# Side work of a Mamba and feed-forward kernel placed in other units

## The chip, the cores and the metric

The kernel runs on one core of a Trainium2 chip. The metric is device time in microseconds (us), the median of several runs; a profiled execution of its own has a time beside them. The core has five engines with queues of their own: PE (TensorE, matrix products), DVE (VectorE), ACT (ScalarE), POOL (GpSimd) and SP (SyncE, which here issues every DMA). They meet through semaphores alone.

## What is computed

For each of 16 batch elements of 512 rows by 256 columns (fp32), with shift, scale and gate rows drawn from a condition vector:

```
h  = layernorm(x) * (1 + ca) + sa
xn = layernorm(h, ln1)
m  = mamba1(xn) + flip(mamba2(flip(xn)))
x  = x + ga * (layernorm(m, ln2) + xn)
h  = layernorm(x) * (1 + cb) + sb
x  = x + gb * ffn(h)        # ternary weights, hidden 1024: silu*gate, gelu, gelu, out

mamba(x): xp, z = split(x @ W_in.T)           # 512 channels each
          xc    = silu(causal conv4(xp) + conv_b)
          dt_lo, B, C = split(xc @ W_xp.T)    # 16, 64, 64
          dt    = softplus(dt_lo @ W_dt.T + dt_b)
          h_t   = exp(dt_t * A) * h_(t-1) + (dt_t * xc_t) * B_t     # 512 x 64 states
          y_t   = h_t . C_t
          out   = ((y + xc * D) * silu(z)) @ W_out.T
```

The recurrence, 512 channels by 64 states by 512 time steps in two directions, is nearly all of the work.

## The kernel before

**Units.** The scan of one batch element is cut into 128 *units*: 8 passes (2 directions by 4 blocks of 128 channels) of 16 groups of 4 states. A unit is 4 tiles of 128 partitions (32 channels by 4 states) by 512 steps, handled in two halves. For each unit ACT computes the decays (`decays`, an exp into `state`), DVE scans twice (`scan`, 128x1024 each, L1278), POOL multiplies the states by C (`read`, twice, L1308), and PE sums them over the states into the bank `y_ps` (`accumulate`, L904). What drives the scan, u times B, is made in two ways. For even units DVE multiplies (`drive`, L1267, at the end of the odd unit before), with B spread by one PE product. For odd units ACT (8 and 4 operations, L1091) and POOL (one, L1375) make `v` in a ring of two, and PE transposes it into the bank pair `driven` (`drive`, L882, two times eight transposes). ACT makes `v` five units ahead in an even unit (first part, after a wait for PE's second drive of the unit after) and the next (second part). The state ring holds four units.

**Order on PE.** In an even unit u: drive(u+1, 0), accumulate(u-1), drive(u+1, 1), spread(u+2), side work of u. In an odd unit: accumulate(u), side work of u. Where u is a multiple of 16, accumulate(u-1) comes first.

**Side work.** Everything else of the network is cut into *steps*, each written into a list for its engine with the unit at whose end it is issued. Each engine runs its list in that fixed order behind its scan work of the same unit, so a step that has to wait stops its whole engine. A mid-body of 128 units has the scan of batch element b, the early and late halves of the feed-forward network of b-1 (`early`, `late`), the projections for the second direction of b (`p1`), and the norm and the projections for the first direction of b+1 (`next`). Bodies: pre (only `next` of element 0), first, 14 times mid, last, tail (the network of the last element with no scan).

**Steps of a projection** (`projection_steps(part, s)`): T0, T1 transpose the input; X0 to X3 project; K0 to K3 are the convolution (two steps each on PE); xc is its silu; BC, CL, BT project to B and C (BC ends with a DVE step that frees its bank); D0 to D3 project dt, whose softplus is ACT's exp, one, ln and DVE's rest (two operations) and dt; ua, ub are POOL's products u = dt * xc; cut is a DVE memset that waits for ub; Z0 to Z3 project z, sz is its silu. UT0 to UT7 transpose u for `v`, one for each pass. Y steps are DVE's: they empty `y_ps` after each pass.

**Steps of the network**: O1a, O1b output projection; `o_` norm, mix, mixed, `n_` norm, N0, N1 transposes, then for each half i: F (8 steps, ACT empties each with two operations), silu, two glu on POOL, H (8 times two quarters), gelu, G (the same), gelu, W (4 steps). `FFN_AT` gives the units at which F, H, G and W begin; `norm_steps` lists stats, aggr (DVE), rstd (POOL, 9 small operations) and norm (ACT). `PRE_AT`, `MIX_AT`, `N_AT`, `X_AT`, `O0_AT`, `UT_AT` place the rest.

**Banks.** Projections, UT and O0 (list PE_P) share one PSUM bank `p_ps`, the network (list PE_Q) shares `q_ps`. `bank_free` makes PE wait until the user before in the same list has been emptied:

```
                by_dve = n in ("BC", "O1a", "O1b", "W0", "W1")
                who = dve_side if by_dve else act_side
                pe.wait_ge(who.sem, who.done(at, p, n))
```

**SP** issues in each unit, in this order: chunks of network weights, the C row of two units on (`load_c`, which waits for POOL's read of this unit), `load_u` for UT, the next pass, stores of B and C and of u and dt (`store_bc`, `store_ud`), weights (`load_wp`, `load_wdt`, `load_wout`), `load_conv`, `load_next`. A wait stops the whole queue.

## Time and profile before

| what | value |
|---|---|
| median of 3 runs | 12781.52 us (12780.62 to 12787.79) |
| profiled execution, its time | 12787.71 us |
| its span, first to last instruction | 12785.9 us |
| mean granted clock of PE | 0.901 |
| busy: DVE | 11921.9 us (93%) |
| busy: POOL | 11371.3 us (89%) |
| busy: ACT | 10826.9 us (85%) |
| busy: PE | 10149.5 us (79%) |
| one batch element (5588.53 to 6363.11) | 774.58 us |

"L1278" is line 1278 of the kernel. In a row of groups, "out<-in" gives the tiles, then the shapes, "x" the count, then busy us, mean ns of one, and the idle time of the engine ahead of it with what ended it. In the timeline a row begins with its start and its duration in us, and the bracket at its end is the idle time ahead of it and what ended that. SPq is SP's queue.

### The profile page before, as it was taken

The page shows a single profiled execution, that of the slowest core. Times are in us where ns is not written, and L with a number is a line of the kernel's source. Part 1 is how long each engine was busy: PE and PEld are TensorE (multiplying, and loading weights), DVE is VectorE, ACT ScalarE, POOL GpSimd, SP SyncE. Part 2 cuts the span into 40 slices and gives each one's busy share as a digit, 9 for nine tenths or more (in the row PEclk, how much of TensorE's full clock was granted, in tenths as well). Part 3 has the DMA queues.
Part 4 walks back from the last instruction along what each step waited for, and adds up shares of the span by engine and source line. Part 5 has one row for each costly group of instructions (what it writes and reads, how often), then busy time and mean ns, then how long its engine had stood idle before and what let it go on. Part 6 is the DMA issues. An engine that isn't in the chain of part 4 may idle for free.

```text
span 12785.9 us, 179504 instructions
## 1 busy us (share of the span) xinstructions
PE 10149.5 (79%) x51484; PEld 5801.2 (45%) x51484; DVE 11921.9 (93%) x7080; ACT 10826.9 (85%) x23460; POOL 11371.3 (89%) x5924
## 2 busy tenths in 40 slices
PE   5667878888787887877878778887878878788777
PEld 2334544444444454544445444454444545444445
DVE  5999999999999999999999999999999999999992
ACT  5788888888888898888888888888888988888882
POOL 4889999999999999999899999999999999999992
PEclk7788989999898998989989899998989989899898
DMA  2223333333333333333333333333333333333332
GB/s 86 81 86 109 123 112 124 126 105 115 114 127 115 114 127 100 131 113 120 123 109 121 110 126 122 109 119 109 127 115 117 123 107 128 111 124 120 110 110 97
DMA packets 610266, 1459.04 MB, mean 114 GB/s; under 512 B 68928, under 2 KB 110032, under 8 KB 604672
## 3 DMA queue, kind: packets, MB, share of 16 engines
q1 hardware_dynamic: 609152, 1446.18, 34.7%
q8 instruction: 456, 7.47, 0.2%
q14 instruction: 658, 5.39, 0.1%
HBM read 1355.09 MB, written 90.83 MB: 113 GB/s over the span
## 4 chain that ended last, share of the span: by engine, by line
PE 29%; issue 25%; DVE 17%; ACT 15%; POOL 10%; DMA 1%; DVEq 0%; SPq 0%; POOLq 0%; ACTq 0%
DVE state L1278 12%; PE driven L882 10%; POOL state L1308 8%; PE y_ps L904 6%; ACT state L1078 5%; ACT v_sb L1091 5%; PE q_ps L837 5%; DVE driven L1267 4%; PE q_ps L824 2%; PE b_ps L872 2%; PE p_ps L745 1%; PE p_ps L769 1%; PE p_ps L753 1%; PE p_ps L760 1%; ACT hid L1061 1%
## 5 line engine op out<-in xcount | busy, mean ns | idle before, releaser
L1308 POOL TENSOR_TENSOR state<-state,c_rep 128x1024 f32<-128x1024 f32 x4096 | 9706.7, 2400 | 962.1 <-DVE state L1278 955.8
L1278 DVE TENSOR_TENSOR_SCAN state<-state,driven 128x1024 f32<-128x1024 f32 x4096 | 9098.6, 2268 | 395.8 <-PE driven L882 384.0
L1078 ACT ACTIVATE state<-ud_rep,cols_sb 128x512 f32<-128x512 f32 x8192 | 5211.4, 710 | 2.9 <-DMA ud_rep<-ud_rows 0.8
L1091 ACT ACTIVATE v_sb<-u_t,b_t 128x128 f32<-128x128 f32 x12288 | 4063.5, 505 | 1260.8 <-PE driven L882 1256.6
L882 PE MATMUL driven<-consts_sb,v_sb 128*128 128x128 f32 x16384 | 2633.3, 314 | 1637.5 <-DVE state L1278 1592.0
L882 PEld LDWEIGHTS driven<-consts_sb,v_sb 128*128 128x128 f32 x16384 | 2129.9, 161 | 3244.5 <-DVE state L1278 2141.1
L904 PE MATMUL y_ps<-state,consts_sb 128*32 128x512 f32 x16384 | 2430.7, 669 | 343.4 <-POOL state L1308 341.4
L1267 DVE TENSOR_TENSOR driven<-ud_rep,b_ps 128x1024 f32<-128x1024 f32 x2048 | 2389.2, 1211 | 18.5 <-DMA ud_rep<-ud_rows 18.5
L837 PE MATMUL q_ps<-hid,wq_sb 128*128 128x256 f32 x7936 | 2043.5, 403 | 146.7 <-ACT hid L1061 70.4
L837 PEld LDWEIGHTS q_ps<-hid,wq_sb 128*128 128x128 f32 x7936 | 1476.7, 196 | 848.9 <-issue 662.1
L1375 POOL TENSOR_TENSOR v_sb<-u_t,b_t 128x512 f32<-128x512 f32 x1024 | 1086.2, 1061 | 37.1 <-issue 24.3
L904 PEld LDWEIGHTS y_ps<-state,consts_sb 128*32 128x32 f32 x16384 | 337.4, 113 | 1166.2 <-POOL state L1308 674.3
L824 PE MATMUL q_ps<-xn_q,wq_sb 128*128 128x256 f32 x1984 | 518.8, 407 | 44.6 <-DMA wq_sb<-in_f 24.1
L753 PE MATMUL p_ps<-u_pad,dt_sb 128*128 128x512 f32 x1024 | 508.7, 621 | 26.2 <-ACT u_pad L980 25.7
L872 PE MATMUL b_ps<-b_parts,onehot 32*128 32x512 f32 x1024 | 523.6, 511 | 0.0
L745 PE MATMUL p_ps<-x_t,wp_sb 128*128 128x512 f32 x1024 | 498.4, 610 | 25.5 <-ACT xc L984 12.6
L824 PEld LDWEIGHTS q_ps<-xn_q,wq_sb 128*128 128x128 f32 x1984 | 373.8, 198 | 222.2 <-issue 99.5
L847 PE MATMUL q_ps<-wq_sb,hid 128*128 128x256 f32 x992 | 274.8, 426 | 71.9 <-ACT hid L1061 68.4
L753 PEld LDWEIGHTS p_ps<-u_pad,dt_sb 128*128 128x128 f32 x1024 | 184.4, 193 | 237.9 <-issue 183.2
L745 PEld LDWEIGHTS p_ps<-x_t,wp_sb 128*128 128x128 f32 x1024 | 187.3, 192 | 222.5 <-issue 148.4
L1056 ACT ACTIVATE hid<-q_ps,cols_sb 128x256 f32<-128x256 f32 x496 | 221.0, 446 | 74.2 <-PE q_ps L837 74.0
L872 PEld LDWEIGHTS b_ps<-b_parts,onehot 32*128 32x128 f32 x1024 | 193.5, 189 | 187.5 <-issue 187.5
(141 smaller groups left out, 5490.2 us busy)
## 6 DMA issues: line engine op xcount, KB each, us to landing
c_rep<-bc_rows SPq DMA_DIRECT2D x2048, 256.0 KB, 3.0
ud_rep<-ud_rows SPq DMA_DIRECT2D x512, 512.0 KB, 4.0
wq_sb<-in_h SPq DMA_DIRECT2D x512, 512.0 KB, 3.7
wq_sb<-in_f SPq DMA_DIRECT2D x128, 512.0 KB, 4.2
wp_sb<-in_win SPq DMA_DIRECT2D x64, 512.0 KB, 4.0
dt_sb<-conv_taps SPq DMA_DIRECT2D x32, 1024.0 KB, 5.2
ud_rows<-u_pad SPq DMA_DIRECT2D x128, 256.0 KB, 3.4
ud_rows<-dt_sb SPq DMA_DIRECT2D x128, 256.0 KB, 3.5
```

What stands on the lines that cost most here:

```text
L753: mm = pe.matmul(p_ps[:], conv_w[:, m, k, :], u_pad[:, m, k:k + T], start=(k == 0), stop=(k == TAPS - 1))
L824: mm = pe.matmul(bank[:, which * TH:(which + 1) * TH], w[:, m % 2, which, k, :], n_t[:, k, i * TH:(i + 1) * TH], start=(k == 0), stop=(k = ...
L837: mm = pe.matmul(bank[:, 0:TH], w[:, k, :], src[:, k, :], start=(k == 0), stop=(k == HC - 1))
L872: pe.matmul(b_ps[:], onehot[k, g % quarter, :], b_parts[d][k, :], start=True, stop=True).then_inc(b_spread, 1)
L882: mm = pe.transpose(driven[:, q % DRIVE_RING, j % 2, tt * P:(tt + 1) * P], v_sb[:, unit // 2 % V_RING, tt, j].rearrange("p e n -> p (e n)" ...
L904: mm = pe.matmul(y_ps[EG * j:EG * (j + 1), :], over_nn, state[:, k % STATE_RING, j, :], start=False, stop=(g == NG - 1))
L1078: ins = act.activation(state[:, unit % STATE_RING, j, :], ud_rep[:, nth % 2, j, 1, :], ACT.Exp, scale=a_neg[:, d, c, j, g:g + 1])
L1091: ins = act.activation(v_sb[:, unit // 2 % V_RING, tt, :, :, n].rearrange("p j e -> p (j e)"), u_t[:, nth % 2, tt, :], ACT.Identity, scale ...
L1267: dve.tensor_tensor(driven[:, h], u_rows(unit)[:, 2 * h:2 * h + 2], b_ps[:].unsqueeze(1).to_broadcast([P, 2, T]), ALU.mult).then_inc(dve_d ...
L1278: dve.tensor_tensor_scan(flat, flat, driven[:, q % DRIVE_RING].rearrange("p j t -> p (j t)"), 0.0, ALU.mult, ALU.add).then_inc(scanned, 1)
L1308: pool.tensor_tensor(part, part, c_rep[:, unit % ROW_RING, :].unsqueeze(1).to_broadcast([P, 2, T]), ALU.mult).then_inc(was_read, 1)
L1375: pool.tensor_tensor(v_sb[:, unit // 2 % V_RING, TT - 1].rearrange("p j e n -> p (j e) n"), u_t[:, nth % 2, TT - 1, :].unsqueeze(2).to_bro ...
```

## The change

Only places change, in the constants at the head and in the offsets of `projection_steps` and of SP's issues that follow them. The projections of `p1` begin at unit 8 instead of 12, those of `next` at 73 instead of 80, and in `next` the blocks X and K come every four units instead of three. D0 to D3 and Z0 to Z3 come in every second unit instead of every unit; DVE's BC step one unit later after ACT's; rest three units after one instead of two, with ln, dt, ua, ub and cut behind it at the same distances as before, so that by units rest and dt stand at 41 and 43 instead of 40 and 42 (`p1`), and at 109 and 111 instead of 108 and 110 (`next`). The `o` norm begins at 7 instead of 8, the last of POOL's pre steps is at 10 instead of 14, mix at 12 instead of 15, the `n` norm at 15 instead of 18, the `x` norm at 59 instead of 64. F, H, G, W of the early half begin at 23, 35, 53, 70 instead of 26, 38, 55, 72, those of the late half at 75, 88, 105, 123 instead of 77, 89, 106, 123. UT0, UT1, UT2, UT5 and UT7 move too. `load_wp` for `next` is tied to `O0_AT` instead of `NEXT_AT`.

```diff
--- before.py
+++ after.py
@@ -46,12 +46,12 @@
 
 
 
-P1_AT, X_AT, NEXT_AT, O0_AT = 12, 64, 80, 68
+P1_AT, X_AT, NEXT_AT, O0_AT = 8, 59, 73, 68
 PASS_AT, FIRST_PASS_AT = (3, 5, 7, 9), (118, 119, 120, 121)
-O1_AT, MIX_AT, N_AT, PRE_AT = 3, 15, 24, (5, 7, 14)
-FFN_AT = (("early", 26, 38, 55, 72), ("late", 77, 89, 106, 123))
-UT_AT = (121, 10, 26, 41, 57, 73, 78, 97)
-GAPS = {"p1": 3, "next": 3}
+O1_AT, O_AT, MIX_AT, N_AT, PRE_AT = 3, 7, 12, 21, (5, 7, 10)
+FFN_AT = (("early", 23, 35, 53, 70), ("late", 75, 88, 105, 123))
+UT_AT = (122, 7, 25, 41, 57, 72, 78, 94)
+GAPS = {"p1": 3, "next": 4}
 
 
 def projection_steps(part, s):
@@ -70,23 +70,23 @@
     act.append((s + 3, part, "xc", 1))
     pe += [(s + 4, part, "BC", 0), (s + 5, part, "BC", 1)]
     act.append((s + 5, part, "BC", 1))
-    dve.append((s + 6, part, "BC", 1))
-    pe += [(s + 7, part, "CL", 0), (s + 8, part, "CL", 1)]
-    act.append((s + 8, part, "CL", 2))
-    pe += [(s + 9, part, "BT", 0), (s + 10, part, "BT", 1)]
-    act.append((s + 10, part, "BT", 1))
+    dve.append((s + 7, part, "BC", 1))
+    pe += [(s + 8, part, "CL", 0), (s + 9, part, "CL", 1)]
+    act.append((s + 9, part, "CL", 2))
+    pe += [(s + 10, part, "BT", 0), (s + 11, part, "BT", 1)]
+    act.append((s + 11, part, "BT", 1))
     for m in range(EC):
-        pe.append((s + 11 + m, part, f"D{m}", 1))
-        act.append((s + 11 + m, part, f"D{m}", 2))
-    act += [(s + 15, part, "exp", 1), (s + 15, part, "one", 1)]
-    dve.append((s + 17, part, "rest", 2))
-    act.append((s + 18, part, "ln", 1))
-    dve += [(s + 19, part, "dt", 1), (s + 22, part, "cut", 1)]
-    pool = [(s + 20, part, "ua", 1), (s + 21, part, "ub", 1)]
+        pe.append((s + 12 + 2 * m, part, f"D{m}", 1))
+        act.append((s + 12 + 2 * m, part, f"D{m}", 2))
+    act += [(s + 19, part, "exp", 1), (s + 19, part, "one", 1)]
+    dve.append((s + 22, part, "rest", 2))
+    act.append((s + 23, part, "ln", 1))
+    dve += [(s + 24, part, "dt", 1), (s + 27, part, "cut", 1)]
+    pool = [(s + 25, part, "ua", 1), (s + 26, part, "ub", 1)]
     for m in range(EC):
-        pe.append((s + 22 + m, part, f"Z{m}", 1))
-        act.append((s + 22 + m, part, f"Z{m}", 1))
-    act.append((s + 26, part, "sz", 1))
+        pe.append((s + 27 + 2 * m, part, f"Z{m}", 1))
+        act.append((s + 27 + 2 * m, part, f"Z{m}", 1))
+    act.append((s + 34, part, "sz", 1))
     return pe, act, dve, pool
 
 
@@ -135,7 +135,7 @@
     for i, name in enumerate(("O0a", "O0b")):
         pe_p += [(O0_AT + 2 * i, "o0", name, 0), (O0_AT + 1 + 2 * i, "o0", name, 1)]
         act.append((O0_AT + 1 + 2 * i, "o0", name, 1))
-    for part, name, s in (("early", "o", MIX_AT - 7), ("early", "n", MIX_AT + 3), ("next", "x", X_AT), ("next", "h", X_AT + 7)):
+    for part, name, s in (("early", "o", O_AT), ("early", "n", MIX_AT + 3), ("next", "x", X_AT), ("next", "h", X_AT + 7)):
         a, b, c = norm_steps(part, name, s)
         pool += a
         act += b
@@ -633,14 +633,14 @@
                         load_u(at, UT_AT.index(unit + 3))
                     if unit % NG in PASS_AT and unit < UNITS - NG and at.kind in SCAN_PARTS:
                         load_pass(at, unit // NG + 1, PASS_AT.index(unit % NG))
-                    if unit == P1_AT + 11 + 3 * GAPS["p1"] and at.has("p1"):
+                    if unit == P1_AT + 12 + 3 * GAPS["p1"] and at.has("p1"):
                         store_bc(at, "p1")
-                    if 0 <= unit - P1_AT - 3 * GAPS["p1"] - 25 < EC and at.has("p1"):
-                        store_ud(at, "p1", unit - P1_AT - 3 * GAPS["p1"] - 25)
-                    if unit == NEXT_AT + 11 + 3 * GAPS["next"] and at.has("next"):
+                    if 0 <= unit - P1_AT - 3 * GAPS["p1"] - 30 < EC and at.has("p1"):
+                        store_ud(at, "p1", unit - P1_AT - 3 * GAPS["p1"] - 30)
+                    if unit == NEXT_AT + 12 + 3 * GAPS["next"] and at.has("next"):
                         store_bc(at, "next")
-                    if 0 <= unit - NEXT_AT - 3 * GAPS["next"] - 25 < EC and at.has("next"):
-                        store_ud(at, "next", unit - NEXT_AT - 3 * GAPS["next"] - 25)
+                    if 0 <= unit - NEXT_AT - 3 * GAPS["next"] - 30 < EC and at.has("next"):
+                        store_ud(at, "next", unit - NEXT_AT - 3 * GAPS["next"] - 30)
                     if unit in FIRST_PASS_AT and at.has("next"):
                         load_pass(at, PASSES, FIRST_PASS_AT.index(unit))
                     if unit == max(P1_AT - 5, 0) and at.has("p1"):
@@ -657,7 +657,7 @@
                         load_wxp(at, "p1")
                     if unit == NEXT_AT and at.has("next"):
                         load_wxp(at, "next")
-                    if unit == P1_AT + 28 + 3 * GAPS["p1"] and at.has("o0"):
+                    if unit == P1_AT + 36 + 3 * GAPS["p1"] and at.has("o0"):
                         load_wout(at)
                     if unit == X_AT - 8 and at.has("next"):
                         load_next(at)
@@ -665,7 +665,7 @@
                         load_skip(at, "o0")
                     if unit == NG * (PASSES - 1) + 4 and at.has("next"):
                         load_skip(at, "next")
-                    if unit == NEXT_AT - 5 and at.has("next"):
+                    if unit == O0_AT + 4 and at.has("next"):
                         load_wp(at, "next", 0)
                     if unit == NEXT_AT - 1 and at.has("next"):
                         store_xn(at)
```

## Rows read from the trace of the kernel before

**Rows 1.** The windows view: one batch; PE, PEld, DVE, ACT, POOL, clock, DMA, GB/s.

```profile
5588.53:6363.11 774.58, 630.42 (x3220) 360.89 (x3216) 744.19 (x441) 675.70 (x1465) 709.37 (x371) 0.91 0.36 117
```

**Rows 2.** The view of groups by shape, window of that batch.

```profile
L1308 POOL TENSOR_TENSOR state<-state,c_rep 128x1024 f32<-128x1024 f32 x256 | 605.4, 2394 | 60.1 <-DVE state L1278 59.8
...
L1078 ACT ACTIVATE state<-ud_rep,cols_sb 128x512 f32<-128x512 f32 x513 | 326.5, 710 | 0.1
L1091 ACT ACTIVATE v_sb<-u_t,b_t 128x128 f32<-128x128 f32 x768 | 254.0, 505 | 71.9 <-PE driven L882 71.7
L882 PE MATMUL driven<-consts_sb,v_sb 128*128 128x128 f32 x1024 | 162.7, 311 | 88.1 <-DVE state L1278 86.1
L904 PE MATMUL y_ps<-state,consts_sb 128*32 128x512 f32 x1028 | 151.3, 663 | 26.1 <-POOL state L1308 26.0
...
L837 PE MATMUL q_ps<-hid,wq_sb 128*128 128x256 f32 x512 | 132.9, 405 | 9.6 <-ACT hid L1056 5.1 <-ACT hid L1061 4.5
...
L1375 POOL TENSOR_TENSOR v_sb<-u_t,b_t 128x512 f32<-128x512 f32 x64 | 67.7, 1059 | 1.8 <-issue 1.8
...
L1226 DVE TENSOR_TENSOR xa<-xa,mod_p 128x1024 f32<-128x1024 f32 x1 | 2.7, 2662 | 0.0
...
L1229 DVE TENSOR_TENSOR xa<-xa,mod_p 128x1024 f32<-128x1024 f32 x1 | 1.5, 1530 | 0.0
```

**Rows 3.** DVE's waits in nine stretches of that batch, in order of time.

```profile
DVE state L1278 <- PE driven L882: 4.5, 8, 1.5
...
DVE b_parts L1244 <- ACT b_parts L992: 2.1, 1, 2.1
...
DVE state L1278 <- PE driven L882: 4.7, 4, 1.9
...
DVE state L1278 <- PE driven L882: 0.7, 2, 0.4
...
DVE state L1278 <- PE driven L882: 3.9, 4, 1.9
...
DVE state L1278 <- PE driven L882: 1.1, 1, 1.1
...
DVE state L1278 <- PE driven L882: 2.7, 4, 1.3
...
DVE u_pad L1248 <- ACT sz L1016: 2.6, 1, 2.6
...
DVE state L1278 <- PE driven L882: 0.8, 2, 0.4
...
DVE dt_sb L1254 <- ACT sz L1019: 0.8, 1, 0.8
...
DVE state L1278 <- PE driven L882: 5.1, 4, 2.7
```

**Rows 4.** Timeline: PE at the second D step, unit 36.

```profile
5805.15 2.07 PE L790 MATMUL p_ps<-sz 16*128 16x512 f32 x2 [4.97 <-ACT u_pad L1010]
```

**Rows 5.** Timeline, units 55 and 56: ACT's gelu with its load, then PE's G00.

```profile
5927.33 1.28 ACT L1061 ACT_TABLE_LOAD   x1
5928.62 1.91 ACT L1061 ACTIVATE hid<-hid 128x2048 f32<-128x2048 f32 x1
...
5930.66 3.78 PE L837 MATMUL q_ps<-hid,wq_sb 128*128 128x256 f32 x8 [4.52 <-ACT hid L1061]
```

**Rows 6.** Timeline of PE, unit 12: a drive after idle time.

```profile
5662.43 1.97 PE L882 MATMUL driven<-consts_sb,v_sb 128*128 128x128 f32 x8 [4.81 <-DVE state L1278]
```

**Rows 7.** Timeline, unit 77: PE's F10.

```profile
6062.03 3.78 PE L824 MATMUL q_ps<-xn_q,wq_sb 128*128 128x256 f32 x8 [1.70 <-DMA wq_sb<-in_f]
```

**Rows 8.** Timeline of DVE: rest's second operation, unit 40, then unit 108.

```profile
5836.46 4.34 DVE L1250 TENSOR_TENSOR dt_sb<-dt_sb,u_pad 128x2048 f32<-128x2048 f32 x1
...
6243.44 2.29 DVE L1250 TENSOR_TENSOR dt_sb<-dt_sb,u_pad 128x2048 f32<-128x2048 f32 x1
```

**Rows 9.** The page's list of DMA issues: x count, KB each, us to landing.

```profile
ud_rows<-u_pad SPq DMA_DIRECT2D x128, 256.0 KB, 3.4
```

## The prediction

> **What bounds the kernel now.** I read the window of one batch first, then the grouped lines of it, then the waits of VectorE (DVE) stretch by stretch, and last the timeline where a wait stood out. All is the batch from 5588.5 to 6363.1 us, one of 16, here for all of them.
>
> DVE is busy 744 of its 774.6 us [rows 1]: it sets the pace, and the rest is about 31 us of waits. Less these and some 42 us of its own side steps, 701 us are left for 64 pairs of units, 11.0 us a pair. An even unit is two scans, an odd unit two scans and two products for the next one. The other engines per pair [rows 2]: POOL 605.4 and 67.7 over 64, 10.5 us, so 0.5 to spare; ACT 326.5 and 254.0 over 64, 9.1 us, 1.9 to spare; PE 162.7 and 151.3 over 64, 4.9 us, and 2.1 for every quarter of a network product (132.9 over 64 such steps; I take projections at the same). Four such steps in a pair make 13 us, more than 11.0. So a side step costs nothing only while its engine's lag stays small, and DVE feels a lag as "waits for PE driven". DVE waits for it in eight stretches, 4.5, 4.7, 0.7, 3.9, 1.1, 2.7, 0.8, 5.1 [rows 3], and outside it 2.1 for b_parts, 2.6 and 0.8 for ACT's sz. By units, in this order: 0 to 22, 34 to 39, 40 to 51, 52 to 69, 70 to 86, 87 to 103, 103 to 111, 112 to 127; the 2.1 is unit 29, the 2.6 and 0.8 units 108 and 110. Everything else is hidden.
>
> **The change, by stretch.** No arithmetic is added or taken away. Each step brings the same instructions and DMAs to another unit, so the sum is of waits, and of DVE steps whose length depends on what POOL does.
>
> Units 34 to 39 (4.7). D0 to D3 each use the one bank p_ps, a unit apart. The second's matmul waits 4.97 us until ACT has emptied the first [rows 4], because the silu with its table loads lies ahead of that in ACT's queue. With D every second unit a whole pair lies between two of them, more than the wait. Left are the two glu steps of POOL (2.4 each against 0.5 to spare), about 0.9. Gain 3.8.
>
> Units 23 to 33 (2.1). DVE's b_parts step moves a unit further from ACT's, so its wait goes. But UT2 now stands at PE's unit 25 and is the next user of p_ps after BC, and this bank is freed by DVE's step, which is at unit 26. PE stops in unit 25 behind it, with the drive of unit 27 queued after: when DVE has done its two scans and the step, it needs UT2 (0.6) and eight transposes (1.2) from PE. 1.8 us come back (from nothing, if UT2 slips in, to 3 on a slow clock). Gain 0.3.
>
> Units 112 to 127 (5.1). Z in every unit beside G makes four quarters in a pair; in every second unit it makes three. gelu1G moves to 121 and W1 stays at 123, so W1 no longer waits for it (same form as [rows 5], gelu in one unit and its reader in the next). sz shares unit 121 with gelu: 9 us of ACT against 1.9, some 0.7 seen. The cut of dt waits for POOL's ub, one unit later than before: 0.5. Other 0.4. Gain 3.5.
>
> Units 0 to 22 (4.5). 1.1 of it, before unit 8, is untouched. The rest is PE at its lower clock (1.2 of 2.4 GHz; granted over the batch 0.91 [rows 1]): after 4.81 us idle the eight transposes take 1.97 us [rows 6], against a mean of 1.27 for eight (162.7 over 128) [rows 2]. Projections now fill these idle places. But the two norms packed closer put POOL steps of 2.4, 3.2, 2.4, 2.4 into units 7 to 13 with 0.5 a pair to spare; POOL falls 4 to 6 us behind, and past about 4 the sums of y hold up the second drive. 1.7 (0 to 4). Gain 1.7.
>
> Units 52 to 69 (3.9). Here I expect a loss. Now G00 waits 4.52 us for gelu0H, runs at the slow clock (3.78) and DVE waits [rows 5]. After, gelu (51) is two units ahead of G00 (53), but sz stands at 53 as well: two table functions, 1.28 + 1.91 + 1.28 each, and Z2 and Z3, in two pairs that hold 1.9 each. ACT's queue from the start of unit 50, with 2.4 for a unit's decays, 2.4 and 1.2 for the two parts of v: first v 8.0 (it waits for the second drive, which ends at 5.6), H07 and Z2 to 10.3, decays and v 13.9, gelu with its loads 18.3, decays and v 23.1. That is 12.1 in the pair of 52; Z3 12.6, decays and v 16.2, sz with its loads 20.7, decays and v 25.5, or 14.5 in the pair of 54, and G00's bank is empty at 14.9. PE has the second half of G00 and a sum of y behind it at 8.7. G01 (55) stands behind that bank and the drive of unit 57 behind G01: one slow quarter 3.8, one drive 1.3, so 20.0, where DVE has done its two scans at 15.4. 4.6 us, 2.6 with PE at 2.4 GHz; I take 4.3. With 1.3 left around the other norm, 5.6. Loss 1.7.
>
> Units 40 to 51 (0.7). The cut waits for ub (1.1). "rest" and "dt" go from even units to odd ones: ln is issued behind ACT's wait for the second drive, so dt waits 0.9; and dt no longer stands behind the cold drives, 0.7. Other 0.3. Loss 2.3.
>
> Units 103 to 111 (0.8 + 2.6 + 0.8). rest no longer waits for sz (2.6, a unit more). dt as above, 1.6. gelu1H goes to 104 with G10 at 105, the form of [rows 5], now with D3 behind it: 2.8. Loss 0.2.
>
> Units 87 to 103 (2.7): pairs with four quarters and POOL's glu coincide less; left 1.8. Gain 0.9.
>
> Units 70 to 86 (1.1): F10 waits 1.70 us for its weights [rows 7], issued behind u_nat and wp_sb in SP's queue. wp_sb's load now goes at unit 72, so this goes; but projections share units 75 to 81 with F10 to F16: 1.4. Loss 0.3.
>
> **Queues.** SP waits in every unit for POOL's read before it loads the next row of C, so all loads move with their units. The next batch's x comes at 51 for 56, the taps at 69 for 76: both are free by then, as their last readers also moved. The last store of u and dt falls into unit 118, in which the first load of the next pass waits for it, 3.4 us [rows 9] against 5.5 of a unit; the next row of C is asked for a unit later. I cost this at nothing; with SP a full unit late it would be 3 us of POOL, once a batch.
>
> **DVE's own steps.** [Rows 8] "rest"'s second operation takes 4.34 us in one place and 2.29 in the other: in the first POOL is reading its states, in the second it had run dry while DVE waited. Likewise the scale of the norm in an even unit 2.66 us and the shift of the same size in an odd one 1.53 [rows 2], because at the end of an odd unit POOL is nearly through. After: both rests at odd ends, 2.59 + 2.29 + 1.05 for POOL's make_v between, 5.9 each, 11.9 for 11.5 now (bounds 9.2 and 13.9); both dt 2.6, for 2.6 and 4.0; mix from an odd to an even unit, +1.3 (bounds 0 and 1.4); scale and shift change parity, +0.6. Sum +0.9 (bounds -2.5 and +4).
>
> The Trainium skill (SBUF — State Buffer, Who interferes with whom) has a DVE instruction with two SBUF inputs and a GpSimd instruction that reads SBUF exclude each other for a whole instruction. The trace agrees: 4.34 is 2.29 and a wait of 2.05. By this rule the moves of mix and shift speak against the change.
>
> **Sum.** Waits: -3.8 - 0.3 - 3.5 - 1.7 + 1.7 + 2.3 + 0.2 - 0.9 + 0.3 = -5.7 us a batch; DVE's steps +0.9; net -4.8. Fifteen and a half such batches (the first lacks the early network): -74 us. The profiled execution took 12787.7 us, 6 above the median of the runs, so 12,708; I say 12,710, 0.56% faster. A measurement of this kernel tells 0.2% (26 us) from no change.
>
> **Rivals.** (1) Slower: ACT's stack at units 51 to 54. Every us that ACT is later there is a us of DVE. It decides when the waits at units 57 and 107, 7.1 in my sum, reach 12. With cold drives after both (two more at 1.97 for 1.1 each) and the D3 and exp behind gelu1H counted in full, they would be 7 and 7, and net +2 a batch: 12,815. For it: the waits of 4.97 and 4.52 [rows 4, 5] come from one table function each. Against: lag is worked off at 1.9 a pair and I may stack too strictly.
> (2) No change: lags only move; DVE has no work less, POOL's 0.5 a pair is the real floor, and what one stretch gives another takes. Net within 1.6 a batch, 12,782. For it: four of my nine terms are losses.
> (3) Larger gain: ACT works its lag off before G00 and G10, and UT2 slips in; only the small waits stay. Terms at 57, 107 and 25 (8.9) shrink to 3: net -10.7, 12,617.
> (4) DVE's pair lock: if POOL is through at each odd end, rest and dt cost 2.29 an operation, 13.7 in all instead of 17.1: 3.4 more a batch, 12,654. The page named above bears on this; its rule alone doesn't say where POOL stands.
>
> **Numbers.** Forecast (12,670 to 12,755) 0.40; rival 4, 0.08; rival 3, 0.12; rival 2, 0.17; rival 1, 0.23. Faster 0.60, same 0.17, slower 0.23. The bounds of the unknown costs (UT2 ±1.5, POOL ±2, unit 57 -2/+3, DVE's steps ±3) give about ±6 a batch, 93 us. The range reaches from rival 3 to just beyond rival 1: 12,610 to 12,840.
>
> **What would show it.** Of the waits after: for b_parts none; a stop of TensorE's UT2 until DVE's b_parts; D's wait for u_pad gone; W1's wait for the gelu gone; G01 waiting for ACT's evacuation; DVE's 4.34 us operations gone or shorter; a dt wait for ln of about 1 us in both directions. The prediction is wrong if DVE's waits in units 52 to 69 or 103 to 111 are far from 5.6 and 4.4, or if POOL's lag dominates units 8 to 20.

## The result, and the profile after

The changed kernel takes 12,808.6 us (median of 13 runs, 12,795.2 to 12,839.5), the kernel before 12,781.0 on the same chip (13 runs, 12,775.2 to 12,800.8): 1.0023 times as long, 95% interval 1.0016 to 1.0031. So it is slower by 0.23%; the forecast was 0.56% faster. The profiled execution spans 12,806.8 us, against 12,785.9 before.

First the same window as in [rows 1], the eighth batch element's body; the columns are those of [rows 1].

```profile
5603.53:6374.94 771.41, 629.02 (x3220) 358.20 (x3216) 741.16 (x442) 674.26 (x1465) 709.22 (x371) 0.92 0.36 118
```

This one body is 3.2 us shorter than before, and the kernel is longer all the same: one body is not enough to read here. Before, middle bodies took 771.0 to 775.6 us, and one 770.7; after, most take 771.1 to 771.5 or 774.4 to 775.0, with single ones at 769.0, 777.1, 778.5 and 781.9. The seventh body (775.0) differs from the eighth mostly in DVE's (VectorE's) waits: 1.3 and 1.9 us more at units 27 and 37, 2.1 less at 77. TensorE (PE) ran the same matmuls at different speeds there: the second drive for unit 27 in 1.79 and 1.09 us, the quarter of H ahead of unit 37 in 3.78 and 3.40, F10 ahead of 77 in 1.99 and 2.87. In the three longest bodies DVE's scale and shift also took 3.2 us each, for 1.7. Summed, the 14 middle bodies are 0.4 us longer each (6.2 in all), the first body 7.4, what lies before it 1.2, the last body and the tail 6.1: 20.9 us, the whole difference of the spans.

DVE's waits in the stretches that answer [rows 3], in order of time (engine and line, what ended the wait: us in total, times, longest):

```profile
DVE state L1278 <- PE driven L882: 4.1, 5, 1.5
...
DVE state L1278 <- PE driven L882: 1.7, 1, 1.7
...
DVE state L1278 <- PE driven L882: 1.7, 2, 1.4
...
DVE state L1278 <- PE driven L882: 3.3, 4, 1.5
DVE dt_sb L1254 <- ACT sz L1019: 1.6, 1, 1.6
...
DVE state L1278 <- PE driven L882: 4.6, 3, 4.0
...
DVE state L1278 <- PE driven L882: 2.6, 2, 2.1
...
DVE state L1278 <- PE driven L882: 1.7, 2, 1.1
...
DVE state L1278 <- PE driven L882: 3.2, 2, 1.7
DVE dt_sb L1254 <- ACT sz L1019: 1.6, 1, 1.6
...
DVE state L1278 <- PE driven L882: 1.4, 2, 0.9
DVE state L1278 <- ACT state L1078: 1.0, 1, 1.0
```

The waits for b_parts and for ACT's `one` (L1016, which writes the tile sz) have gone; two waits for ln (L1019) of 1.6 us stand where one of 0.8 stood, and one single wait of 4.0 us has come in units 52 to 69. On the whole-span page the scans' idle time for PE went from 384.0 to 419.9 us:

```profile
L1278 DVE TENSOR_TENSOR_SCAN state<-state,driven 128x1024 f32<-128x1024 f32 x4096 | 9100.3, 2268 | 456.0 <-PE driven L882 419.9
```

Because bodies differ, I added up all idle time of DVE by unit over the 14 middle bodies of both traces (without the wait ahead of unit 0's first scan, 0.5 us in both). Mean us per body:

| units | before | after | difference | forecast |
|---|---|---|---|---|
| 0 to 22 | 4.7 | 4.1 | -0.7 | -1.7 |
| 23 to 33 | 2.6 | 2.5 | -0.1 | -0.3 |
| 34 to 39 | 4.6 | 2.3 | -2.3 | -3.8 |
| 40 to 51 | 1.1 | 4.8 | +3.8 | +2.3 |
| 52 to 69 | 3.7 | 5.5 | +1.8 | +1.7 |
| 70 to 86 | 0.9 | 1.4 | +0.5 | +0.3 |
| 87 to 102 | 3.4 | 2.3 | -1.1 | -0.9 |
| 103 to 111 | 3.7 | 5.2 | +1.5 | +0.2 |
| 112 to 127 | 3.9 | 2.9 | -1.0 | -3.5 |
| sum | 28.6 | 30.9 | +2.3 | -5.7 |
| DVE's own side steps | 42.6 | 40.3 | -2.3 | +0.9 |

**Where the two largest new waits arise.** DVE's timeline at units 41 to 45 (start, us, engine, line, operation, count, and in brackets the idle time before and what ended it):

```profile
5850.94 2.51 DVE L1248 SCALAR_TENSOR_TENSOR u_pad<-sz,u_pad 128x2048 f32<-128x2048 f32 x1
5853.48 3.01 DVE L1250 TENSOR_TENSOR dt_sb<-dt_sb,u_pad 128x2048 f32<-128x2048 f32 x1
5856.42 6.63 DVE L1278 TENSOR_TENSOR_SCAN state<-state,driven 128x1024 f32<-128x1024 f32 x3
5864.17 2.29 DVE L1278 TENSOR_TENSOR_SCAN state<-state,driven 128x1024 f32<-128x1024 f32 x1 [1.12 <-PE driven L882]
5866.38 2.33 DVE L1267 TENSOR_TENSOR driven<-ud_rep,b_ps 128x1024 f32<-128x1024 f32 x2
5870.34 2.29 DVE L1254 TENSOR_TENSOR dt_sb<-dt_sb,sz 128x2048 f32<-128x2048 f32 x1 [1.63 <-ACT sz L1019]
```

and PE's:

```profile
5858.75 1.97 PE L882 MATMUL driven<-consts_sb,v_sb 128*128 128x128 f32 x8 [6.37 <-DVE state L1278]
5860.65 1.93 PE L904 MATMUL y_ps<-state,consts_sb 128*32 128x512 f32 x8
5862.51 1.62 PE L882 MATMUL driven<-consts_sb,v_sb 128*128 128x128 f32 x8
...
5874.88 1.97 PE L882 MATMUL driven<-consts_sb,v_sb 128*128 128x128 f32 x8 [5.48 <-DVE state L1278]
5876.78 1.94 PE L904 MATMUL y_ps<-state,consts_sb 128*32 128x512 f32 x8
```

While DVE does rest at the end of odd unit 41, PE has nothing to do. Its first drive for 43 starts only once DVE has scanned the first half of unit 42, after 6.37 us of idleness, and takes the 1.97 us of [rows 6]; such a drive is called cold below, one of 1.09 us warm. Drive, sum of y and drive take 5.4 us to 5864.1; DVE's scans last until 5863.05. Behind dt at the odd end of unit 43, and its wait for ln, the same comes again for unit 45: 5.48 us of idleness, cold drives, a wait of 1.4 us in the mean.

ACT at units 51 to 53, and PE's G01:

```profile
5922.14 1.28 ACT L1061 ACT_TABLE_LOAD   x1
5923.43 1.91 ACT L1061 ACTIVATE hid<-hid 128x2048 f32<-128x2048 f32 x1
...
5931.48 0.63 ACT L1024 ACTIVATE sz<-p_ps 128x512 f32<-128x512 f32 x1
...
5935.88 1.28 ACT L1027 ACT_TABLE_LOAD   x1
5937.18 1.91 ACT L1027 ACTIVATE sz<-sz 128x2048 f32<-128x2048 f32 x1
5939.10 1.28 ACT L1078 ACT_TABLE_LOAD   x1
...
5945.22 0.44 ACT L1056 ACTIVATE hid<-q_ps,cols_sb 128x256 f32<-128x256 f32 x1
```

```profile
5945.78 3.55 PE L837 MATMUL q_ps<-hid,wq_sb 128*128 128x256 f32 x8 [6.29 <-ACT hid L1056]
```

ACT empties G00's bank at 5945.22, behind gelu, Z3 and sz; PE stands still for 6.29 us, and unit 57's scan waits 4.02 us for the drive behind G01. This is the stack that the prediction computed (4.3 us; the mean over the 14 middle bodies is 4.1, against 1.8 before).

### The profile page after: what moved, and what is told of

It is laid out like the page before. It is cut to its first block, busy times and chain, and to the rows that moved or that the text cites. A ratio compares the mean times of both kernels' runs of the same rounds, so it can differ in the third digit from the quotient of the medians.

```text
span 12806.8 us, 179490 instructions
## 1 busy us (share of the span) xinstructions
PE 10218.9 (80%) x51484; PEld 5803.5 (45%) x51484; DVE 11891.5 (93%) x7080; ACT 10803.2 (84%) x23446; POOL 11343.4 (89%) x5924
## 4 chain that ended last, share of the span: by engine, by line
issue 25%; PE 24%; ACT 18%; DVE 16%; POOL 13%; DMA 2%; DVEq 0%; POOLq 0%; SPq 0%; ACTq 0%
DVE state L1278 11%; POOL state L1308 10%; PE driven L882 8%; ACT state L1078 7%; ACT v_sb L1091 6%; PE y_ps L904 5%; DVE driven L1267 4%; PE q_ps L837 3%; PE q_ps L824 2%; PE p_ps L745 1%; PE p_ps L753 1%; PE b_ps L872 1%; DMA c_rep<-bc_rows 1%; POOL hid L1359 1%; ACT hid L1061 1%
## 5 line engine op out<-in xcount | busy, mean ns | idle before, releaser
L1278 DVE TENSOR_TENSOR_SCAN state<-state,driven 128x1024 f32<-128x1024 f32 x4096 | 9100.3, 2268 | 456.0 <-PE driven L882 419.9
L904 PE MATMUL y_ps<-state,consts_sb 128*32 128x512 f32 x16384 | 2463.1, 677 | 408.3 <-POOL state L1308 403.4
L1267 DVE TENSOR_TENSOR driven<-ud_rep,b_ps 128x1024 f32<-128x1024 f32 x2048 | 2390.1, 1212 | 18.1 <-DMA ud_rep<-ud_rows 18.1
L837 PE MATMUL q_ps<-hid,wq_sb 128*128 128x256 f32 x7936 | 2098.1, 410 | 226.2 <-ACT hid L1056 155.5
L837 PEld LDWEIGHTS q_ps<-hid,wq_sb 128*128 128x128 f32 x7936 | 1510.9, 200 | 955.9 <-issue 737.6
L1375 POOL TENSOR_TENSOR v_sb<-u_t,b_t 128x512 f32<-128x512 f32 x1024 | 1139.3, 1113 | 45.5 <-issue 30.6
L847 PE MATMUL q_ps<-wq_sb,hid 128*128 128x256 f32 x992 | 248.9, 395 | 3.6 <-DMA wq_sb<-in_w 3.6
```

The source lines that it names most:

```text
L837: mm = pe.matmul(bank[:, 0:TH], w[:, k, :], src[:, k, :], start=(k == 0), stop=(k == HC - 1))
L904: mm = pe.matmul(y_ps[EG * j:EG * (j + 1), :], over_nn, state[:, k % STATE_RING, j, :], start=False, stop=(g == NG - 1))
L1267: dve.tensor_tensor(driven[:, h], u_rows(unit)[:, 2 * h:2 * h + 2], b_ps[:].unsqueeze(1).to_broadcast([P, 2, T]), ALU.mult).then_inc(dve_d ...
L1278: dve.tensor_tensor_scan(flat, flat, driven[:, q % DRIVE_RING].rearrange("p j t -> p (j t)"), 0.0, ALU.mult, ALU.add).then_inc(scanned, 1)
L1375: pool.tensor_tensor(v_sb[:, unit // 2 % V_RING, TT - 1].rearrange("p j e n -> p (j e) n"), u_t[:, nth % 2, TT - 1, :].unsqueeze(2).to_bro ...
```

## The experiments

Each kernel was timed in five rounds beside the kernel before. Its medians in the three groups of experiments were 12,777.8, 12,782.5 and 12,782.9 us, so the medians of different groups can be set side by side within some 5 us. Each experiment has 4 to 11 runs. The ratios are to the kernel before; the changed kernel ("changed", 12,808.6 us) has 1.0023 (1.0016 to 1.0031). Waits by unit are means over the 14 middle bodies.

### One edit each, from the changed kernel

**rest to cut a unit sooner** (in `projection_steps`):

```
-    dve.append((s + 22, part, "rest", 2))
-    act.append((s + 23, part, "ln", 1))
-    dve += [(s + 24, part, "dt", 1), (s + 27, part, "cut", 1)]
-    pool = [(s + 25, part, "ua", 1), (s + 26, part, "ub", 1)]
+    dve.append((s + 21, part, "rest", 2))
+    act.append((s + 22, part, "ln", 1))
+    dve += [(s + 23, part, "dt", 1), (s + 26, part, "cut", 1)]
+    pool = [(s + 24, part, "ua", 1), (s + 25, part, "ub", 1)]
```

> The changed kernel with rest, ln, dt, ua, ub and cut of both projections a unit sooner, so that rest and dt stand at the end of even units (40 and 42, 108 and 110) as they did before; nothing else moves. Theory A (place in the pair: ln is issued behind ACT's wait for the second drive, and the products of the next odd unit run cold while PE stands): the waits of units 43 and 45 (1.25 and 1.37 us) and 111 (1.36) shrink to 0.4 each or less, the two waits for ln (1.63, 1.64) go, the second operation of rest goes back to 4.3 us in at least one place (+1 to +2 a batch); net -3.8 us a batch, about -59 us: 12,750. Theory B (lags only move, POOL has no slack): the waits are found again in the next units or in the longer rest; net within 1 us a batch, 12,795 to 12,820.

Measured: 12,720.2 us, ratio 0.9957 (0.9943 to 0.9970), 88 us less than changed and 58 less than before. DVE's waits fell from 4.8 to 0.8 us in units 40 to 51 and from 5.2 to 2.5 in 103 to 111; its side steps grew by 2.7. The same place in its trace, DVE and then PE:

```profile
5821.21 4.45 DVE L1278 TENSOR_TENSOR_SCAN state<-state,driven 128x1024 f32<-128x1024 f32 x2
5825.59 2.57 DVE L1254 TENSOR_TENSOR dt_sb<-dt_sb,sz 128x2048 f32<-128x2048 f32 x1
5828.08 4.45 DVE L1278 TENSOR_TENSOR_SCAN state<-state,driven 128x1024 f32<-128x1024 f32 x2
```

```profile
5823.54 1.97 PE L882 MATMUL driven<-consts_sb,v_sb 128*128 128x128 f32 x8 [7.34 <-DVE state L1278]
5825.44 1.94 PE L904 MATMUL y_ps<-state,consts_sb 128*32 128x512 f32 x8
5827.31 1.56 PE L882 MATMUL driven<-consts_sb,v_sb 128*128 128x128 f32 x8
```

PE is as slow as before (5.3 us from the first drive to the end of the second), but dt now lies between the scans of unit 42 and those of 43, and covers it: no wait. In the kernel before it was so too: 7.54 us of idleness, a first drive of 1.97 us, and dt at the end of unit 42 covered it. Theory A holds in kind, and gave too little (59 us). Twelve of the 14 middle bodies now take 767.6 to 768.4 us.

**Only rest and ln a unit sooner**, dt and what follows left at the odd units:

```
-    dve.append((s + 22, part, "rest", 2))
-    act.append((s + 23, part, "ln", 1))
+    dve.append((s + 21, part, "rest", 2))
+    act.append((s + 22, part, "ln", 1))
     dve += [(s + 24, part, "dt", 1), (s + 27, part, "cut", 1)]
```

> The changed kernel with only rest and ln a unit sooner (40 and 41, 108 and 109); dt, ua, ub and cut stay at the odd units 43 and 111 and after. It splits the gain of 88 us that all of them had. Theory A (half is the wait for ln, half the cold drives behind a long stop of VectorE at an odd end): ln's 1.63 and 1.64 go, the waits at 43 and 111 (1.25 and 1.36) go with rest, the wait at 45 (1.4) behind dt stays, rest's operation is 4.3 us instead of 3.0 twice: -1.6 x 2 - 1.3 x 2 + 1.0 x 2, -3.9 us a batch, -60 us: 12,748. Theory B (ln alone): -3.3 + 2.0 = -1.3 us a batch, 12,788.

Measured: 12,779.0 us, ratio 0.9996 (0.9987 to 1.0005): 30 us of the 88. Both waits for ln are gone, the wait at 45 fell to 0.4, but those at 43 and 111 remained at 1.0 us each where they had been 1.3 and 1.4, and 0.6 and 1.2 us more appeared at 57 and 61. Theory A is refuted in its split: what lies at the odd end of unit 41 is not what makes unit 43 wait. Nor does dt at the odd end of unit 43 make unit 45 wait 1.4 us by itself: without the wait for ln in front of it PE is idle for 3.91 us, not 5.48, and DVE waits 0.42:

```profile
5857.30 1.61 PE L882 MATMUL driven<-consts_sb,v_sb 128*128 128x128 f32 x8 [3.91 <-DVE state L1278]
```

```profile
5862.02 2.29 DVE L1278 TENSOR_TENSOR_SCAN state<-state,driven 128x1024 f32<-128x1024 f32 x1 [0.42 <-PE driven L882]
```

The larger part, 59 us, comes with dt at the even end. Of the 4.1 us a body by which the waits of these two kernels differ, 2.4 stand where dt does (units 40 to 51 and 103 to 111) and 2.4 in units 52 to 86, with 0.7 the other way elsewhere; why the units from 57 on wait less, these traces don't settle.

**UT2 ahead of BC:**

```
-UT_AT = (122, 7, 25, 41, 57, 72, 78, 94)
+UT_AT = (122, 7, 22, 41, 57, 72, 78, 94)
```

> The changed kernel with TensorE's UT2 three units sooner (unit 22 for 25), ahead of BC in the one bank p_ps, its load moved along. Theory A (the bank): DVE's waits at unit 27 (1.69 and 0.55 us) go to 0.5 or less together, nothing takes their place, -1.8 us a batch or -28 us: 12,780. Theory B (PE is late in 25 to 27 because of the load of quarters and network steps alone): the wait at 27 stays over 1.2 us, the time within 10 us of the changed kernel. In between: CL takes the place of UT2 behind DVE's step and stops a unit later, half of the gain.

In the changed kernel PE stood behind DVE's b_parts step as forecast:

```profile
5762.94 0.65 PE L784 MATMUL p_ps<-consts_sb,u_nat 128*128 128x128 f32 x4 [1.70 <-DVE b_parts L1244]
```

Measured: 12,792.2 us, ratio 1.0012 (1.0003 to 1.0021), an interval that overlaps that of the changed kernel. The waits at 27 are gone, and unit 29 got 1.3 and unit 31 some 0.5: of 2.2 us of waits at 27 four fifths were given back. That is neither theory: the wait moved on by one pair. In the first body, which has no early network beside it, the stretch is 2.8 us shorter.

**sz of p1 at unit 59:**

```
-    act.append((s + 34, part, "sz", 1))
+    act.append((s + (40 if part == "p1" else 34), part, "sz", 1))
```

> The changed kernel with sz of the one projection (p1) six units later, at 59 instead of 53, so that the gelu of unit 51 is alone ahead of G00 and G01. Theory A (ACT's stack of two table functions in two pairs): the wait at unit 57 falls from 4.1 us to between 0.5 and 1.7, sz at 59 costs 0.5 at most, -2.4 us a batch or -37 us: 12,771. Theory B (the gelu and the four quarters in a pair do it, sz is worked off): the wait at 57 stays above 3 us, the time within 10 us. Theory C (only moved): 57 falls, but units 59 to 64 get 2 us of new waits, the time within 10 us.

Measured: 12,738.2 us, ratio 0.9966 (0.9952 to 0.9979), 70 us less than changed. The waits of the stretch 52 to 69, 4.6 us in the changed kernel's body:

```profile
DVE state L1278 <- PE driven L882: 1.1, 3, 0.5
```

No wait at all is left at unit 57, and 0.4 at 59. Theory A, and more than it said: here a gelu alone, two units ahead of its reader, costs nothing; one step of the projection in the pair behind it costs 4.5 us a body.

**H1 a unit sooner**, so that its gelu has two units to G10:

```
-FFN_AT = (("early", 23, 35, 53, 70), ("late", 75, 88, 105, 123))
+FFN_AT = (("early", 23, 35, 53, 70), ("late", 75, 87, 105, 123))
```

> The changed kernel with the sixteen half products of H1 a unit sooner (87 to 102 instead of 88 to 103) and so its gelu at 103, two units ahead of G10 at 105. Theory A (G10 waits for the gelu of the unit ahead of it): the wait at 107 falls from 2.0 us to 0.8 or less, -1.2 us a batch or -19 us: 12,789. Theory B (the wait at 107 is exp and D3 in ACT's queue): it stays over 1.5 us. Theory C: H10 in unit 87 then waits for POOL's second glu step (86) and the gain is given back there: 0.

Measured: 12,786.4 us, ratio 1.0008 (0.9999 to 1.0017); not clearly apart from the changed kernel's interval. Unit 107 waits 0.4 us for 2.0, as A has it, and unit 89 waits 3.5 for 1.5, as C has it. PE there:

```profile
6112.88 1.94 PE L904 MATMUL y_ps<-state,consts_sb 128*32 128x512 f32 x8 [3.73 <-POOL state L1308]
6114.74 3.78 PE L837 MATMUL q_ps<-hid,wq_sb 128*128 128x256 f32 x8
6118.32 2.33 PE L745 MATMUL p_ps<-x_t,wp_sb 128*128 128x512 f32 x4
```

The sum of y comes late, behind POOL, which had two glu steps (2.4 us each) in these units, and it comes cold; and now a quarter of H stands behind it, ahead of the drive.

### The spacing undone

**D0 to D3 in consecutive units**, where the kernel before had them (34 to 37, 102 to 105):

```
-        pe.append((s + 12 + 2 * m, part, f"D{m}", 1))
-        act.append((s + 12 + 2 * m, part, f"D{m}", 2))
+        pe.append((s + 15 + m, part, f"D{m}", 1))
+        act.append((s + 15 + m, part, f"D{m}", 2))
```

> The changed kernel with D0 to D3 of both projections in consecutive units again, at 34 to 37 and 102 to 105, exactly where the kernel before had them; exp, rest and all else stay. Theory A (the wait of the second D for the one bank, 4.97 us in the kernel before, was a wait of DVE of 2.5 us): stretch 34 to 39 goes from 35.4 back to about 38.0 us, the other projection adds 0 to 0.5, together +2.8 us a batch or +43 us: 12,850. Theory B (only moved lags): what units 34 to 39 lose, the units without D at 31 to 33 and 40 to 41 give back; within 12 us.

Measured: 12,834.8 us, ratio 1.0041 (1.0027 to 1.0055), 26 us more. As a time this is barely clear of noise (the interval of the changed kernel reaches 1.0031, and the runs overlap), but in the trace unit 107 waits 5.5 us for 2.0, 4.5 or more in each of the 14 bodies. The place was not the one that either theory named. Units 34 to 39 wait 2.0 us, less than the 2.3 of the changed kernel. All of the loss is in 103 to 111 (8.5 us for 5.2), where D2 now shares unit 104 with gelu1H; the waits of that stretch, and PE at G10:

```profile
DVE state L1278 <- PE driven L882: 6.7, 3, 5.1
```

```profile
6254.12 3.78 PE L837 MATMUL q_ps<-hid,wq_sb 128*128 128x256 f32 x8 [4.50 <-ACT hid L1061]
6257.83 2.07 PE L790 MATMUL p_ps<-sz 16*128 16x512 f32 x2
```

**The kernel before with the network part alone**: mix, its norm and the early network three units sooner, D still in 34 to 37:

```
-O1_AT, MIX_AT, N_AT, PRE_AT = 3, 15, 24, (5, 7, 14)
-FFN_AT = (("early", 26, 38, 55, 72), ("late", 77, 89, 106, 123))
+O1_AT, MIX_AT, N_AT, PRE_AT = 3, 12, 21, (5, 7, 10)
+FFN_AT = (("early", 23, 35, 53, 70), ("late", 77, 89, 106, 123))
```

with `o` at `MIX_AT - 5`.

> The kernel before with one part of the change alone: mix, its norm and the early network three units sooner (PRE 5, 7, 10, o's norm at 7, MIX 12, N 21, early 23, 35, 53, 70); both projections, D and Z in consecutive units, x's norm and the loads as before. Theory A (it was silu0 at unit 34, beside D0 to D3, that made DVE wait in 34 to 39, not the closeness of the D's): 34 to 39 falls from 38.0 to about 35.4 us, 0 to 22 by 1.2, and gelu0H now stands two units ahead of G00 (the wait of 1.7 at 57 stays or falls by 1, as sz at 49 is near it): -4 us a batch or -62 us: 12,720. Theory B (the D's a unit apart do it): 34 to 39 stays at 37.5 or more; -1 to -2 us a batch, 12,755.

Measured: 12,746.8 us, ratio 0.9973 (0.9961 to 0.9985), 36 us less than before. Units 34 to 39 wait 1.8 us where the kernel before had 4.6; those of one body, against 4.7 in [rows 3]:

```profile
DVE state L1278 <- PE driven L882: 1.7, 2, 1.3
```

So theory A's mechanism: silu0 left unit 34, and the D's could stay a unit apart. In the kernel before, ACT's queue shows it: silu0 with its load lies ahead of the two operations that empty the first D's bank, for which PE waits 4.97 us [rows 4]:

```profile
5800.74 1.28 ACT L1050 ACT_TABLE_LOAD   x1
5802.03 1.91 ACT L1050 ACTIVATE hid<-hid 128x2048 f32<-128x2048 f32 x1
5803.85 0.67 ACT L1009 ACTIVATE dt_sb<-p_ps,cols_sb 128x512 f32<-128x512 f32 x1
5804.42 0.68 ACT L1010 ACTIVATE u_pad<-p_ps,cols_sb 128x512 f32<-128x512 f32 x1
```

This edit moves POOL's two glu steps away from the D's as well; no run moves silu0 alone. Its gain was too high by 26 us, since units 70 to 86 gave back 1.2 (1.5 at unit 71), and the wait at 57 (1.8 before, 0.3 here) came back as 1.1 at 53. This one part is worth having by itself.

**Z0 to Z3 in consecutive units** (46 to 49, 114 to 117), sz unmoved:

```
-        pe.append((s + 27 + 2 * m, part, f"Z{m}", 1))
-        act.append((s + 27 + 2 * m, part, f"Z{m}", 1))
+        pe.append((s + 27 + m, part, f"Z{m}", 1))
+        act.append((s + 27 + m, part, f"Z{m}", 1))
```

> The changed kernel with Z0 to Z3 in consecutive units, at 46 to 49 and 114 to 117, sz where it is (53, 121). Theory A (as the prediction costed it: four quarters in a pair beside G are what units 112 to 127 suffered from): +1.5 to +3.5 us a batch at 112 to 127; at unit 57 ACT has no Z2 and Z3 in its stack, -1.3 us; net +0.2 to +2.2 a batch, 12,811 to 12,843. Theory B (the spacing of Z gives nothing at 112 to 127, 93.7 against 93.1 us in the two traces): +0.6 there, -1.3 at 57, net -0.7 a batch, 12,798.

Measured: 12,774.6 us, ratio 0.9992 (0.9982 to 1.0001), 34 us less than changed (one run of eleven, far off all others at 15,954.6 us, does not move the median). Units 112 to 127 wait 2.5 us, less than the 2.9 with Z spaced, so the gain the prediction had put there isn't there. Units 52 to 69 went from 5.5 to 3.9. Theory B in kind, and more in size.

### Together

**Two edits**: rest to cut a unit sooner, and sz of p1 at 59.

> The changed kernel with the first and third edits together: rest to cut a unit sooner, and sz of p1 at 59. Theory A (waits are local and add up): the two gains of 88 and 70 us add to 158: 12,650. Theory B (one floor, POOL's half us a pair): less than two thirds of the sum, 12,700 or more.

Measured: 12,646.0 us, ratio 0.9888 (0.9873 to 0.9903): 163 us less than changed, where the two gains alone add to 158. Waits sum to 18.9 us a body, for 30.9. Theory A.

**The same with Z in consecutive units:**

> The kernel with two edits (rest to cut a unit sooner, sz of p1 at 59; 12,646) with Z0 to Z3 in consecutive units again. Theory A (the closeness of the Z's is worth nothing by itself; it saved 34 us only because Z2 and Z3 then stood outside ACT's stack of gelu and sz at 51 to 54): here the stack is gone, so 0 +- 10 us: 12,636 to 12,656. Theory B (Z beside H0 is cheaper than Z beside G0 anyway): -20 us or more.

Measured: 12,672.3 us, ratio 0.9911 (0.9897 to 0.9925), 26 us more, with no run of either kernel inside the range of the other's. Both theories missed. With the stack at 51 to 54 gone, the spacing of Z is a gain of 26 us; with the stack there, a loss of 34. The 26 are less sure than the 34: four and five runs, and the intervals overlap (0.9873 to 0.9903 and 0.9897 to 0.9925). In the traces nine of 14 bodies of the kernel with two edits last 764.2 to 764.9 us, as twelve do here; the gap comes from five shorter ones there (760.6 to 762.3) and two longer ones here (768.0 and 771.8).

**All four edits** (UT2 at 22 and H1 at 87 as well):

> The changed kernel with all four edits: rest to cut a unit sooner, sz of p1 at 59, UT2 at 22, H1 a unit sooner. Theory A (they add up): the gains of 88, 70, 17 and 22 us add to 197: 12,612. Theory B: UT2's and H1's small gains were a matter of which batches ran cold, and vanish beside the others: within 10 us of the kernel with two edits.

Measured: 12,673.1 us, ratio 0.9912 (0.9898 to 0.9925), 27 us more than with two, again with no overlap of the runs. Neither theory: the two small edits, each at or below what can be told alone, cost something beside the others (the intervals overlap here too). By unit, the wait moved to 89 costs 1.7 us, and 107 gives back 1.4 while 105 takes 0.6; UT2's 1.7 at 27 came back as 1.3 and 0.5 at 29 and 31.

**Two edits, and sz of the other projection at 124:**

```
-    act.append((s + (40 if part == "p1" else 34), part, "sz", 1))
+    act.append((s + (40 if part == "p1" else 37), part, "sz", 1))
```

> The kernel with two edits with sz of the other projection three units later too, at 124 instead of 121, so that gelu1G of unit 121 is alone. Theory A (the waits of units 124 and 125, 0.57 and 0.97 us for ACT's decays, and 0.45 at 123 come from gelu and sz in one unit): these 2.0 us go to 0.5, and sz costs 0.4 elsewhere: -1.1 us a batch or -17 us: 12,629. Theory B: they move with sz to units 127 to 3 of the next batch: within 8 us.

Measured: 12,624.8 us, ratio 0.9873 (0.9858 to 0.9888), 21 us less than with two edits, near theory A's 12,629; the runs of the two overlap (12,612.5 to 12,633.4, and 12,623.2 to 12,652.1), so as a time it isn't clear of noise. In the trace units 112 to 127 wait 1.6 us for 2.5; 124 and 125, which had waited for ACT's decays, gave up 1.5 us and 127 took 0.5. The end of one body:

```profile
DVE state L1278 <- PE driven L882: 0.9, 2, 0.5
DVE state L1278 <- ACT state L1078: 0.6, 1, 0.6
```

This version beats both kernels: 1.27% faster than the kernel before, and the body of the same batch element takes 764.43 us:

```profile
5527.77:6292.20 764.43, 627.60 (x3220) 355.22 (x3216) 744.01 (x441) 675.45 (x1465) 713.46 (x371) 0.92 0.37 119
```

Waits fell to 17.2 us a body, with DVE's own side steps as before (42.7).

## Why the prediction was wrong, by its own steps

It moved the other way: 12,710 was forecast, 12,808.6 came, inside the range. The waits were taken 8.0 us a body too low (+2.3 measured for -5.7), DVE's own steps 3.2 too high (-2.3 for +0.9). The steps that failed are the gain of units 112 to 127 (3.5 forecast, 1.0 measured), the gain of units 34 to 39 (3.8, 2.3), the loss of rest and dt at odd ends in units 40 to 51 and 103 to 111 (2.5, 5.3), the gain of units 0 to 22 (1.7, 0.7), the end of F10's wait for its weights (1.7 before, 2.2 after), and bodies other than the middle ones, taken to behave like them. Of the 95 us between the forecast -74 and the spans' +20.9, 73 lie in the middle bodies and 22 outside.

**Units 40 to 51 and 103 to 111** (+2.3 and +0.2 forecast, +3.8 and +1.5 measured): the right mechanism, mis-sized, and one place of it overlooked. That dt "no longer stands behind the cold drives" was priced at 0.7 for 43 and again for 111, where 1.25 and 1.4 came; that dt at the odd end, with its wait for ln, makes the drives of 45 cold in turn (1.4; 0.4 once the wait for ln is gone) was not in the sum. The wait for ln was priced at 0.9 and came as 1.6, twice. Against that the cut waited 0.1 where 1.1 was forecast, and unit 107 waits 2.0, not 2.8. The first edit, its half and the kernel before show the reason: PE idles and comes back slow in either arrangement, but a step of DVE at an even end lies ahead of the scans that need the slow drives, one at an odd end doesn't. That placement, the waits for ln included, costs 88 us, 5.7 a body. It is enough for the sign: with it undone the kernel is 0.43% faster than before. It is not the only one that is: with sz of p1 moved instead, the kernel is 0.34% faster.

**Units 52 to 69** (+1.7; +1.8 measured): right, cause, place and size. The 4.3 at unit 57 was 4.1. Taking sz away took it away whole. What the prediction missed is that this loss belonged to the change's sz, not to its early gelu, and could be had back for 0.4 us at unit 59.

**Units 34 to 39** (-3.8; -2.3): the right culprit, the wrong edit. The silu with its table loads did lie ahead of the D's evacuation [rows 4]; with silu0 at 31, and the glu behind it, the wait is gone with the D's a unit apart (1.8 left) or two (2.3), so the spacing of D had no part in it. That spacing was worth 3.3 us a body of waits near gelu1H (26 us by the medians, at the edge of noise), where nothing had been forecast for it. "Left" was 2.3, not 0.9.

**Units 112 to 127** (-3.5; -1.0): the term that missed by most, 2.5. The base was one body's 5.1 where the mean is 3.9; the spacing of Z, to which the gain was given, saves nothing there; and gelu1G and sz in unit 121, costed at 0.7, hold up ACT's decays, 1.4 us at 124 and 125, which the last experiment removes.

**Units 0 to 22** (-1.7; -0.7): two waits for cold drives remain, at 5 and 11, 1.4 us each in the mean. **Units 23 to 33** (-0.3; -0.1): right; the wait for b_parts gone, UT2's stop 1.7 where 1.8 was forecast, and 0.6 more at unit 27. **Units 87 to 102**: within 0.2. **Units 70 to 86** (+0.3; +0.5): near in size, but by luck. F10's wait for its weights was to go, since wp_sb's load no longer stands ahead of theirs; it stayed, 2.2 us in the mean of the 14 bodies after 1.7 before, and unit 77 waits behind it:

```profile
6064.06 2.87 PE L824 MATMUL q_ps<-xn_q,wq_sb 128*128 128x256 f32 x8 [2.81 <-DMA wq_sb<-in_f]
```

With the network part alone (W from 70, F10 at 77) no body shows that wait; before and after, F10 stands five units behind the start of W, there seven. Which of the loads' conditions it is, no run separates.

**DVE's own steps** (means over the 14 middle bodies). rest took 11.8 us a body for 11.9 forecast, but before it was 12.2, not 11.5: -0.4 for +0.4. dt 4.6, before 5.8: -1.2 for -1.4. mix did not lengthen: 1.31 us, before 1.87 (1.3 to 1.6 in twelve bodies, 4.9 in two), so -0.6 for +1.3. scale and shift evened out, 2.1 each, -0.1 for +0.6: the body answers [rows 2] with

```profile
L1229 DVE TENSOR_TENSOR xa<-xa,mod_p 128x1024 f32<-128x1024 f32 x1 | 1.7, 1735 | 0.0
L1226 DVE TENSOR_TENSOR xa<-xa,mod_p 128x1024 f32<-128x1024 f32 x1 | 1.7, 1693 | 0.0
```

The prediction took the parity of the unit for what sets these lengths. All fourteen traces show what does: how much POOL's running instruction has left when the step begins. Where that is more than 0.15 us, rest's second operation and dt last it plus 2.15 us (652 of 652 cases; 2.29 with POOL idle), scale and shift last it plus 1.08 (413 of 413). At rest's odd end 0.86 us were left, hence the 3.01; at mix's even end 0.2. DVE's multiplication for the drive (L1267), which has one operand in PSUM, takes 1.20 to 1.23 whatever POOL does. The Trainium skill (SBUF — State Buffer, Who interferes with whom) calls the port pair that the two engines share an exclusive lock; the traces agree, and the rule says nothing of parity.

**Outside the middle bodies.** The factor 15.5 assumed that the first body behaves like half a middle one. It grew by 7.4 us, where waits grew by 3.7 in units 23 to 33 (moving UT2 gave 2.8 us of these back) and by 3.7 in units 40 to 51. The last body and the tail took 6.1 more, of which 2.4 after the last scan unit; these I did not trace to a cause.

**The rivals.** Rival 1 (12,815) has nearly the time measured, by other waits than its own: those at 57 and 107 sum to 6.1 us, not 12. It came out near by chance. Rival 2, that lags only move and POOL's 0.5 a pair is the floor, is refuted: two edits took 12 us a body off the waits, and what they gave alone (158 us) they gave together (163). It describes the two small edits (UT2, H1), whose gains came back in other units. Rivals 3 and 4 did not occur; rest at an odd end took 3.0 us, neither 2.29 nor 4.34.

Open: why the spacing of Z, undone beside the two edits, costs 26 us. By unit it is waits at 3, 9, 48, 57, 117, 119 and 123, 0.5 to 1 us more at each, against somewhat less at 5, 11 and 16, and no experiment separates them.

## What to carry to other kernels

- In a pipeline whose units come in pairs with different feeding, a side step's place within the pair can be worth more than its distance from its neighbours (here 88 us, against 26 and -34 for the two spacings). Put a long step of the pacing engine where it covers the slow hand-over, not behind it.
- Two table functions of ACT in neighbouring pairs formed a stack here (gelu at 51, sz at 53: 4.1 us at unit 57), though the first was two units ahead of its reader. List them by unit and try a free pair after each.
- A wait that goes when four things move may belong to one of them. Before crediting an edit, ask which other part of the same change also takes the cause away. And average over all bodies: one body's 5.1 us was 3.9 in the mean.

## What the runs showed that was not expected

- The body's length jumps by 3.4 us (771.3 or 774.7 us in the changed kernel, by turns and without a pattern), and PE runs the same matmuls at different speeds in different bodies (the second drive for unit 27 in 1.79 or in 1.09 us). With rest and dt at even ends, 12 of 14 bodies lie within 0.8 us.
- Two large edits added up (163 us for 158), while the spacing of Z was worth -34 or, less surely, +26 us, depending on where sz and rest stood.
- Four of DVE's side steps with both operands in SBUF (rest's second operation, dt, scale, shift) wait out POOL's running instruction: their length is what that instruction has left plus a fixed time, to within 0.01 us.
